# Up to four of the next group's row-maximum matmuls issued between the chunks of each MLP's first half

## What is computed

```python
for layer in (0, 1, 2):
    mod = silu(c) @ w_mod + b_mod                       # 6 vectors of 144
    h = modulate(layernorm(x), mod)
    q, k, v = heads(h @ w_qkv + b_qkv)                  # 16 heads of 9 channels
    attn = softmax(q @ k.T * 9 ** -0.5)                 # 512 x 512 for each head
    x = x + gate * (merge(attn @ v) @ w_proj + b_proj)
    h = modulate(layernorm(x), mod)
    x = x + gate * mlp(h)      # gelu(h @ w1 + b1) @ w2 + b2, 144 -> 576 -> 144
                               # layer 0: 4 experts, top 2 of them weighted per token
U, _ = qr(P)                   # P 144 x 64
R = expm(skew(silu(cond) @ W.T + b))                    # 64 x 64 for each batch
out = x + ((x @ U) @ R - x @ U) @ U.T
```

## Time and profile before

| | us |
|---|---|
| three runs, median (lowest to highest) | 943.3 (941.29 to 946.74) |
| the profiled execution | 947.13 |
| its span, first to last instruction | 945.4 |
| PE busy in it | 764.5 |
| DVE busy | 601.7 |
| ACT busy | 381.3 |
| POOL busy | 167.5 |
| mean granted clock of PE | 0.872 |

### The profile page before, as it was taken

One profiled execution on the slowest core, in us unless ns is written; L12 is line 12 of the kernel. 1 busy time (PEld: TensorE's weight loads), 2 busy tenths in 40 slices (PEclk: granted clock), 3 DMA queues, 4 the chain that ended last, 5 costly groups with the idle time before them and its releaser, 6 DMA issues.

```text
span 945.4 us, 11211 instructions
## 1 busy us (share of the span) xinstructions
PE 764.5 (81%) x3571; PEld 443.5 (47%) x3571; DVE 601.7 (64%) x1770; ACT 381.3 (40%) x682; POOL 167.5 (18%) x352
## 2 busy tenths in 40 slices
PE   5697989878997699788757987979886879979746
PEld 1353544346654344456443444535443545446335
DVE  3367887773238957842578677477788477784332
ACT  0221564433533344344333432416443446646511
POOL 5401021321111100213321002121003021021020
PEclk9999999987997568889975786779998999999957
DMA  3210101010120000011100000010000100000000
GB/s 85 67 34 6 37 8 41 18 40 1 46 64 21 1 23 11 12 32 49 47 18 1 23 12 1 12 32 0 24 12 12 32 1 24 12 12 1 13 1 12
DMA packets 22716, 21.24 MB, mean 22 GB/s; under 512 B 4832, under 2 KB 17016, under 8 KB 22659
## 3 DMA queue, kind: packets, MB, share of 16 engines
q1 hardware_dynamic: 22610, 20.52, 8.3%
q10 hardware_dynamic: 48, 0.02, 0.0%
HBM read 13.62 MB, written 0.61 MB: 15 GB/s over the span
## 4 chain that ended last, share of the span: by engine, by line
PE 57%; DVE 33%; issue 5%; ACT 3%; POOL 1%; DMA 0%; SPq 0%; DVEq 0%; ACTq 0%; POOLq 0%
PE m_bank L1362 10%; DVE row_max L911 10%; PE o_bank L1384 8%; PE s_bank L1345 7%; PE d_bank L1499 7%; PE m_bank L1551 3%; PE d_bank L1445 2%; PE m_bank L1371 2%; PE d_bank L1490 2%; DVE h_tok L970 2%; DVE gram_rows L1152 2%; PE d_bank L1493 1%; PE d_bank L1491 1%; PE d_bank L1492 1%; PE d_bank L1402 1%
## 5 line engine op out<-in xcount | busy, mean ns | idle before, releaser
L752 ACT ACTIVATE probs<-s_bank 128x512 f32<-128x512 f32 x384 | 222.8, 598 | 394.9 <-PE s_bank L1345 391.8
L911 DVE TENSOR_REDUCE row_max<-m_bank 128x1 fp32r<-128x512 f32 x384 | 255.6, 686 | 125.2 <-PE m_bank L1362 119.4
L1362 PE MATMUL m_bank<-k_pad,q_t 128*128 128x512 f32 x348 | 178.5, 527 | 47.4 <-DVE row_max L911 14.1
L1345 PE MATMUL s_bank<-q_t,k_pad 128*128 128x512 f32 x384 | 175.7, 461 | 2.6 <-ACT probs L752 1.6
L1362 PEld LDWEIGHTS m_bank<-k_pad,q_t 128*128 128x128 f32 x348 | 73.7, 216 | 123.4 <-issue 38.1
L1384 PE MATMUL o_bank<-probs,v_aug 128*32 128x512 f32 x768 | 119.7, 700 | 4.1 <-DVE o_tok L929 3.3
L1345 PEld LDWEIGHTS s_bank<-q_t,k_pad 128*128 128x128 f32 x384 | 83.3, 217 | 23.2 <-ACT probs L752 11.0
L1499 PE MATMUL d_bank<-w,g_act 128*128 128x144 f32 (+1 forms) x480 | 61.8, 287 | 8.7 <-issue 8.7
L1499 PEld LDWEIGHTS d_bank<-w,g_act 128*128 128x128 f32 (+1 forms) x480 | 59.5, 190 | 14.6 <-ACT g_act L821 13.1
L674 POOL TENSOR_TENSOR h_tok<-h_tok,mod 128x144 f32<-128x144 f32 x48 | 24.3, 507 | 220.4 <-DVE h_tok L970 220.4
L1551 PE MATMUL m_bank<-gram_rows,ident 64*64 64x208 f32 (+42 forms) x128 | 41.7, 415 | 4.8 <-DVE gram_rows L1152 4.2
(11 more groups left out here) (239 smaller groups left out, 1178.3 us busy)
## 6 DMA issues: line engine op xcount, KB each, us to landing
k_pad<-k_t SPq DMA_DIRECT2D x96, 64.0 KB, 2.0
raw_a<-in_L_cond_w_dram SPq DMA_DIRECT2D x10, 288.0 KB
w<-in_L_cond_w_dram SPq DMA_DIRECT2D x10, 288.0 KB
w_rows<-in_L_cond_W_dram SPq DMA_DIRECT2D x8, 141.8 KB
raw_d<-in_L_cond_w_dram SPq DMA_DIRECT2D x30, 36.0 KB
x_tok<-in_x_dram SPq DMA_DIRECT2D x2, 288.0 KB, 4.0
w<-in_L_cond_W_fc_dram SPq DMA_DIRECT2D x2, 288.0 KB
raw_a<-in_L_cond_W_fc_dram SPq DMA_DIRECT2D x2, 288.0 KB
```

What stands on the lines that cost most here:

```text
L752: act.activation(probs[:, n % PROBS, :], s_banks[n % S_BANKS][:, :], ACT.Exp, scale=HD ** -0.5)\
L911: dve.tensor_reduce(row_max[:, grp % 2, t, MAXROW + 32 * j:MAXROW + 32 * j + 1], bk[:, :], AX.X, ALU.max).then_inc(drained, 1)
L1345: pe.matmul(s_banks[n % S_BANKS][:, :], k_pad[:, grp % PADS, j, kt * P:(kt + 1) * P], q_t[:, par, g, :], start=True, stop=True).then_inc(s ...
L1362: ins = pe.matmul(bk[:, :], q_t[:, par, g, t * P:(t + 1) * P], k_pad[:, grp % PADS, j, :], start=True, stop=True)
```

## The change

`tile_plan` replaces `MAX_SHARE`. It keeps the shares of 2, 2, 1, 1, ... for the steps, but counts what is already done, and puts up to four tiles (`BURST`) inside the step that holds an MLP's first slot: PE issues one behind each of the chunks 0 to 3. `UPS` counts those slots for each step. The tiles run ahead of the schedule, so the steps after an MLP have none until the schedule catches up:

| block | bursts (step: tiles) | steps left without a tile |
|---|---|---|
| 0 | 84: 4, 86: 4, 88: 1 | 85 to 93 |
| 1 | 148: 4, 150: 4, 152: 1 | 149 to 157 |
| 2 | 213: 4 | 214 to 217 |
| 3 | 278: 4 | 279 to 282 |
| 4 | 360: 4 | 361 to 364 |

That is 30 tiles of 384; their number, their operands and their order are as before. The MLPs of steps 90 and 154, and the last one, have no burst. On DVE the four reductions stand in the MLP's first slot, ahead of the wait for its second half.

```diff
+def ups_at():
+    kinds = [(st[0], i) for block in range(BLOCKS) for st in stages(block) for i in range(len(BANKS_OF[st[0]]))]
+    left, out = iter(kinds), []
+    for slots in SLOTS:
+        out.append(sum([next(left) == ("mlp", 0) for _ in range(slots)]))
+    return out
+UPS = ups_at()
...
-MAX_SHARE = [2, 2] + [1] * (GSTEPS - 4) + [0, 0]
 TURN_AT = GSTEPS - 2
-def max_tiles(step):
-    at = sum(MAX_SHARE[:step % GSTEPS])
-    return [divmod(i, GRP) for i in range(at, at + MAX_SHARE[step % GSTEPS])]
+BURST = 4
+def tile_plan():
+    before, inside = [[] for _ in range(BLOCKS * STEPS)], [[] for _ in range(BLOCKS * STEPS)]
+    for first in range(0, (BLOCKS * G - 1) * GSTEPS, GSTEPS):
+        done = 0
+        for k in range(TURN_AT):
+            want = max(0, min(GSTEPS, k + 3) - done)
+            before[first + k] = [divmod(i, GRP) for i in range(done, done + min(want, 2))]
+            done += min(want, 2)
+            more = min(BURST * UPS[first + k], GSTEPS - done)
+            inside[first + k] = [divmod(i, GRP) for i in range(done, done + more)]
+            done += more
+        assert done == GSTEPS
+    return before, inside
+TILES, BURST_TILES = tile_plan()
...
 # DVE, mlp
                 down = ring.take(), ring.take()
+                while burst:
+                    take_max(*burst.pop(0))
                 yield
...
 # DVE, the loop over steps
                 def fill_once():
-                    if len(maxima) == len(max_tiles(n)):
+                    while burst:
+                        take_max(*burst.pop(0))
+                    if len(maxima) == len(TILES[n]):
                         next_max()
                 if n:
+                    for tile in BURST_TILES[n - 1]:
+                        burst.append(((n - 1) // GSTEPS + 1, *tile, mring.take()))
...
                         next(woven)
+                    while burst:
+                        take_max(*burst.pop(0))
...
 # PE, mlp, behind the fourth matmul of a chunk
                         .then_inc(s["up_full"], 1)
+                    if burst:
+                        max_scores(*burst.pop(0))
...
 # PE, the loop over steps
-                    for t, j in max_tiles(n):
+                    for t, j in TILES[n]:
                         max_scores(grp + 1, t, j)
+                    burst[:] = [(grp + 1, *tile) for tile in BURST_TILES[n]]
...
                     next(woven)
+                while burst:
+                    max_scores(*burst.pop(0))
```

More of the change, by code:

```diff
@@ L856, in _ @@
                 if n:
+                    for _ in BURST_TILES[n - 1]:
+                        mring.take()
                     for _ in range(SLOTS[n - 1]):
@@ L906, in _, with take_max @@
                         .then_inc(s["c_wide"], 1)
-            def take_max(grp, t, j):
-                bk, drained, _ = mring.take()
+            def take_max(grp, t, j, taken=None):
+                bk, drained, _ = taken or mring.take()
                 dve.wait_ge(s["max_full"], seen.next("max_full"))
@@ L1062, in gate @@
                 yield
+            burst = []
             def mlp(m, blk):
```

4 lines of the change are left out of this document (2 added, 2 removed).

## The result

The changed kernel takes 934.6 us (median of 20 runs, 929.0 to 944.2 us but for one), the kernel before 942.1 us beside it. The ratio is 0.9913, 95% interval 0.989 to 0.9935: 8.2 us faster (6.1 to 10.4). Ratios here compare runs in the fast state alone, which leaves out two of the 20 (944.2 us, and 1141.2 us at a mean granted clock of 0.575); the two medians are 7.5 us apart. A second timing gave 0.9908 (0.9875 to 0.9942). The profiled execution took 937.49 us, its span 935.8, at a mean granted clock of 0.868.

What follows compares the result with a forecast made beforehand. PE was taken to bound the MLPs and DVE the tails behind them. Block terms -1.4, -2.2, -1.1, -1.2 and -0.4 sum to -6.3 us, from the 943.3 us median to 937.0 us; range 931.5 to 943.0 us.

Steps and rivals of the forecast that it cites:

- PE full in the MLPs, DVE in the tails: Across the MLPs and the stretches behind them: a reduction costs nothing inside an MLP and its full 0.69 us in a tail.
- A burst costs 0.23 us per tile: Inside the MLPs: each maximum matmul adds 0.23 us on PE, 0.9 us for four, at full clock.
- Block 0, -1.4 us: Block 0: bursts +2.1, seven matmuls out of PE-bound steps -1.6, a reduction ahead of `moe` -0.7, the tail -1.2 us.
- Block 1, -2.2 us: Block 1: bursts +1.3 and +1.2, matmuls -1.2, three reductions ahead of waits -0.7 each, two in the tail -1.4 us.
- The term +1.3: Block 1's first burst: PE waits for banks, chunk 2 starts 0.9 us later, and later burst matmuls partly run at half clock.
- the tail's -1.4: Block 1's tail: two reductions fewer, 1.37 us long, were to shorten it by 1.4 us.
- Block 2, -1.1 us: Block 2: burst +0.9, two matmuls in PE-bound steps -0.5, the residual wait at mods -0.25, two tail reductions -1.3 us.
- Block 3, -1.2 us: Block 3: burst +0.9, no PE gain before the tail, and the tail's four reductions, 2.17 us, taken away.
- Block 4, -0.4 us: Block 4: burst +0.5, two of its matmuls fitting PE's 0.80 us gelu wait; four matmuls fewer in PE-bound steps, -0.9 us.
- The clock eats it: Rival, chance 0.18: work behind each tail stays at half clock, 30 matmuls losing 0.20 us each, 6 us; result 943.0 us.
- The tails give half back: Rival, chance 0.15: the four tails yield half of 6.8 us, as POOL, PE or dependent DVE operations still hold; 940.4 us.
- Bursts stop PE inside the MLPs: Rival, chance 0.07: maximum matmuls waiting for banks stop the chunks; four of nine MLPs cost 25 us, giving 962 us.

## Why the prediction was right, step by step

The forecast of -6.3 us stands beside -8.2 (6.1 to 10.4), and beside -6.5 and -7.3 in the sum of stretches. The sign, the mechanism and the size of the total held. Of its five terms block 1 and block 4 were 1 us too small each and block 2 was 1 us too large; block 0's can't be read. The kernel without the 30 tiles splits blocks 1 to 4 in two: taking the tiles out of their steps gave 8.5 us where 9.8 was said, and the bursts cost 2.6 to 3.0 where 4.8 was said. Both sides were put too high, and that they nearly cancel is luck. Of the prediction's own signs, "tails shorter by 1.2 to 2.2 us" failed in all four (0.66 to 0.92, and 2.87). The lower end of its range, 931.5, isn't worked out either: 2 us of clock and the 1.3 of the burst lead to 933.7.

**PE full in the MLPs, DVE in the tails: right.** The kernels with short reductions, and with the bursts behind the second half, show it from both sides.

**A burst costs 0.23 us per tile: right.** Steps 86, 150 and 278 are 0.92, 0.90 and 0.92 us longer than without the tiles; 0.93 was the term. (Step 213 is 1.15 us longer, 0.24 of it a later start of the MLP, which waits for `h_d`.) In block 4, 0.46 against 0.5, since PE waited for gelu anyway. Not seen was that the same tiles cost nothing 1 us later, ahead of the second half, although the 0.73 us stand ahead of each second half in the trace of before.

**Block 0, -1.4 us: not settled.** The three readings of its new code are 84.53, 83.34 and 83.17, the two of the old code 85.13 and 81.79. The `mods` wait went from 1.41 to 1.11 us; about 0.7 was said. Other work on DVE was late there too. In the changed kernel's profile the second half of the mods matmuls ran at half clock (the last two rows here, 1.8 us against 0.99 in the row ahead of them; before, the third pair took 1.50), and the tail's granted clock was 0.61 after 0.74. The first MLP also had PE wait 0.64 us for a bank drained by a solver step (first row), which I had excluded; in the second profile of the same kernel it doesn't:

```profile
221.28 0.80 PE L1399 MATMUL m_bank<-k_pad,q_t 128*128 128x512 f32 x1 [0.64 <-DVE gram_rows L1183]
...
274.79 0.99 PE L1438 MATMUL d_bank<-ada_a,c_wide_a 128*128 128x432 f32 x2 [1.11 <-DVE moe L1110]
...
276.78 1.81 PE L1438 MATMUL d_bank<-ada_a,c_wide_a 128*128 128x432 f32 x2
...
278.52 1.80 PE L1439 MATMUL d_bank<-ada_d,c_wide_d 17*128 17x432 f32 x2
```

**Block 1, -2.2 us: it gained 3.2.** The step on the first burst was seen in every detail except what it led to. PE after, from the reduction that frees the bank to the start of the second half:

```profile
401.65 0.68 DVE L938 TENSOR_REDUCE row_max<-m_bank 128x1 fp32r<-128x512 f32 x1
...
402.39 0.54 PE L1399 MATMUL m_bank<-k_pad,q_t 128*128 128x512 f32 x1 [2.85 <-DVE row_max L938]
...
404.86 0.63 PE L1527 MATMUL d_bank<-h_hi,ff_hi 128*128 128x512 f32 x1
...
406.14 0.40 PE L1530 MATMUL d_bank<-h_d,ff_d 96*128 96x512 f32 x1
...
409.58 5.15 PE L1538 MATMUL d_bank<-w,g_act 128*128 128x144 f32 x40 [0.73 <-issue]
```

The first chunk starts at 398.36 here and at 402.35 before, so 3.99 us have to be added to compare: PE stopped until 406.38 on the old clock (said: 406.4), chunk 2 began at 408.85 (said: 408.8). But half clock lasted only for the first of these two windows after, against the second, of before (length, PE, PEld, DVE, ACT, POOL, granted clock, DMA):

```profile
402.70:406.20 3.50, 3.50 (x10) 2.69 (x9) 3.22 (x11) 1.78 (x3) 2.52 (x3) 0.51 0.00 0
```

```profile
406.69:413.52 6.83, 5.49 (x12) 3.37 (x12) 3.76 (x10) 2.92 (x6) 3.27 (x3) 0.50 0.00 0
```

PE is busy for all of the 3.50 us after, and for 5.49 of 6.83 before. The term +1.3 should have been -0.6: step 148 is 16.70 and 16.73 us long, 17.28 in the kernel without the 30 tiles (17.62 before, with the tile of step 149 in it). The Trainium skill ("TensorE: Matmul & The Clock Gate", Part 1) has it that activity releases the throttle. These rows agree in so far as the busier stretch is the shorter one at 1.2 GHz. The prediction had used that rule as an argument against the change; in this MLP it may have worked for it, which no run tests.

Two other terms of the block fit: step 153's wait of 0.73 us is gone, and step 156 is 0.83 us shorter for the reduction ahead of the last `moe` and a matmul. The third MLP's wait for `moe` is still 1.39 us after 1.45, because matmuls ahead of it left as well; from the second half before it to its start it is 7.44 us after 7.97, so 0.53 was gained where 0.7 was put for the reduction alone.

What failed is the tail's -1.4, and with it the "nothing" that the prediction put for POOL. The tail's 0.66 us are step 156's, so its two reductions brought nothing at the end. DVE does reach the norm 1.82 us earlier, counted from the score matmul of step 156 (4.82 after 6.64). But from the first statistics to the normalisation (L970, now L997) it then takes 6.62 us after 5.46. POOL prepares weights beside it, and operations of four columns that take 0.16 us elsewhere take 1.25 beside POOL's of 1.40: twice after (first rows), once before (last two rows), where POOL's first one fell on the statistics.

```profile
463.15 0.16 DVE L917 SCALAR_TENSOR_TENSOR nwt<-nwt,rstd 128x4 f32<-128x4 f32 x1
463.18 1.40 POOL L674 TENSOR_TENSOR lay_lo<-raw_a,lay_hi 128x576 fp32r<-128x576 f32 x1
463.35 1.25 DVE L918 TENSOR_TENSOR nwt<-nwt,rstd 128x4 f32<-128x4 f32 x1
...
465.26 1.40 POOL L678 TENSOR_TENSOR lay_d<-raw_d,lay_d 32x576 fp32r<-32x576 f32 x1
465.44 1.25 DVE L918 TENSOR_TENSOR nwt<-nwt,rstd 128x4 f32<-128x4 f32 x1
```

```profile
471.00 1.40 POOL L653 TENSOR_TENSOR lay_d<-raw_d,lay_d 32x576 fp32r<-32x576 f32 x1
471.18 1.25 DVE L891 TENSOR_TENSOR nwt<-nwt,rstd 128x4 f32<-128x4 f32 x1
```

In block 0, with POOL idle, the same chain lasts 3.56 or 3.57 us in all 13 profiles; in block 1 it lasts 5.41 to 5.64 in three and 6.50 to 6.64 in the other ten. That POOL's work is what stretches it is read from this; no run moved it. PE's last wait is 8.28 us after 8.21:

```profile
470.07 1.09 PE L1408 MATMUL m_bank<-ident_r,row_max 128*128 128x128 f32 x4 [8.28 <-DVE rot L1256]
```

**Block 2, -1.1 us: it gained 0.1.** Here the mis-sized terms are -0.5 and -0.25 for the matmuls. The kernel with short reductions is 1.3 us shorter in this stretch, as the DVE term had it, and leaving the matmuls out too brings nothing more (38.25 and 38.33). The steps behind this MLP end with PE waiting for DVE, so a matmul less only lengthens the wait, from 3.55 to 4.62 us:

```profile
622.29 0.80 PE L1399 MATMUL m_bank<-k_pad,q_t 128*128 128x512 f32 x1 [4.62 <-DVE lu L1219]
```

**Block 3, -1.2 us: it gained 1.1 and 0.7.** A wait at one of the four maximum matmuls (before, first row) is gone with the matmul, and PE at the norm's end waits 4.44 us (after, second row) in place of 4.83. The tail is 2.87 us shorter, more than the 2.17 of the term, and steps 284 to 286, behind it, gave 0.8 us back to half clock (1.3 in the second profile).

```profile
755.32 0.51 PE L1362 MATMUL m_bank<-k_pad,q_t 128*128 128x512 f32 x1 [1.84 <-DVE row_max L911]
```

```profile
752.44 0.35 PE L1591 MATMUL m_bank<-lu,ident 64*64 64x7 f32 x2 [4.44 <-DVE lu L1219]
```

**Block 4, -0.4 us: it gained 1.5.** The step that failed is that its reductions were counted at nothing. Ahead of the turn in step 366, DVE had two additions of the MLP's result and then two reductions to do, and PE stood for them. Before, on DVE and PE:

```profile
875.39 0.46 DVE L1024 TENSOR_TENSOR x_tok<-x_tok,gated 128x288 f32<-128x288 f32 x1
875.88 1.29 DVE L911 TENSOR_REDUCE row_max<-m_bank 128x1 fp32r<-128x512 f32 x2
...
877.27 0.63 PE L1371 MATMUL m_bank<-ident_r,row_max 128*128 128x128 f32 x4 [1.19 <-DVE row_max L911]
```

After, the same matmul starts without a wait for DVE:

```profile
868.65 0.66 PE L1408 MATMUL m_bank<-ident_r,row_max 128*128 128x128 f32 x4
```

The rows of before had that price in them: a tail needs no norm to be one, a turn that waits for the last maximum is enough.

**The rivals.** *The clock eats it* is right in places (block 0's tail, steps 284 to 286) and wrong in block 1's first MLP; no loss shows in the total of either timing. *The tails give half back* came true in block 1's tail, where all of the 1.4 us went, though in the norm's own chain beside POOL and not in gaps that now stand empty. Over all four it is wrong: they are 5.3 us shorter, and 6.8 was the whole. *Bursts stop PE inside the MLPs*: it happened in the two MLPs behind a gate, for 0.64 us (in one profile of the two) and 2.85 us (in both), and nowhere else.

## What to carry to other kernels

Price work that is to be moved by who is the bound where it stands and where it goes; then look in the goal for an idle gap of the engine. Here 0.73 us ahead of each second half took three tiles for nothing, while the same tiles cost 0.7 us between the chunks. Then look at what the moved work left ahead of the goal: one tile that took a bank behind long work of DVE held up PE for 2.5 us, and a plan without it and two others was 3 to 4 us shorter there. And look at what the freed chain then runs beside: block 1's norm started 1.8 us earlier and lost 1.2 of it beside POOL's work. Where half clock falls by chance moves the time by more than such a part is worth, so compare stretches between fixed instructions over several profiles before you trust a median.
